# Cross attention's probability-value products as three fp16 products, their halves made by GpSimd and VectorE, on one Trainium2 core

## The reference

```python
x = _layernorm(x + self_attention(x))            # 8 heads of 16, biases, blocks of 64 tokens
x = _layernorm(x + cross_attention(x, ctx))      # 16 heads of 8, masked softmax, 64 keys
x = _layernorm(x + ffn(x))                       # 8 experts of 512, silu, top 2 by a router
```

```python
scores = jnp.einsum('bhqd,bhkd->bhqk', qh * SCALE, kh)
scores = jnp.where(mask[:, None, :, :], jnp.float32(-1000000000.0), scores)
attn = jax.nn.softmax(scores, axis=-1)
out = jnp.einsum('bhqk,bhkd->bhqd', attn, vh)    # the product that the change touches
```

## Time and profile before

| | us |
|---|---|
| median of 3 runs (lowest, highest) | 1054.99 (1054.93, 1057.35) |
| the profiled execution: its own time | 1055.75 |
| its span, first to last instruction | 1054.0 |
| PE busy | 897.6 (85%) |
| DVE busy | 790.4 (75%) |
| ACT busy | 711.0 (67%) |
| POOL busy | 429.1 (41%) |

### The profile page before, as it was taken

How to read it: one execution, slowest core, us unless ns; L and a number is a source line. 1 busy time by engine, 2 the same in 40 slices (tenths; PEclk the granted TensorE clock), 3 DMA queues, 4 the chain that set the end, 5 groups by cost and what they waited for, 6 DMA issues and landing times. The chain is left out here.

```text
span 1054.0 us, 30689 instructions
## 1 busy us (share of the span) xinstructions
PE 897.6 (85%) x11092; PEld 800.9 (76%) x11093; DVE 790.4 (75%) x2208; ACT 711.0 (67%) x1194; POOL 429.1 (41%) x527
## 2 busy tenths in 40 slices
PE   2898999898799989899898988893079999999990
PEld 1777777777588878788887877782079999999990
DVE  3688888888667887888887778777547777777771
ACT  3678777776577766767676756651058878878881
POOL 3133443344301110111212115565717777777773
PEclk9999999999799998999998989996589999999995
DMA  5960000000100000000000100010132332332210
GB/s 162 216 114 21 20 10 20 20 20 11 26 14 14 14 14 14 14 12 12 12 12 0 23 3 25 29 41 21 52 70 58 72 74 65 73 73 58 61 32 0
DMA packets 103725, 42.26 MB, mean 40 GB/s; under 512 B 58290, under 2 KB 99516, under 8 KB 103668
## 3 DMA queue, kind: packets, MB, share of 16 engines
q1 hardware_dynamic: 98676, 32.95, 15.0%
q0 software_dynamic: 4992, 8.54, 2.5%
HBM read 20.69 MB, written 16.57 MB: 35 GB/s over the span
## 5 line engine op out<-in xcount | busy, mean ns | idle before, releaser
L1118 DVE TENSOR_REDUCE mx<-psum 128x8 bf16<-128x512 f32 x192 | 132.2, 689 | 85.6 <-PE psum L539 82.7
L923 ACT ACTIVATE pr<-psum 128x512 f32<-128x512 f32 x192 | 114.2, 595 | 79.3 <-PE psum L618 78.9
L386 POOL TENSOR_SCALAR ve<-mv 128x4 f32<-128x4 f32 x55 | 15.8, 288 | 336.9 <-DVE mv L1276 322.9
L515 POOL DMA_INDIRECT out_dram<-X,dest x92 | 123.7, 1345 | 61.1 <-ACT X L1026 43.0
L627 PE MATMUL psum<-ident,pr 128*128 128x128 f32 x768 | 123.1, 284 | 29.7 <-ACT pr L923 29.6
L927 ACT ACTIVATE pt<-psum 128x512 f32<-128x512 f32 x192 | 113.8, 592 | 32.8 <-PE psum L627 32.1
L645 PE MATMUL psum<-vz_cross,pt 128*128 128x36 f32 x1024 | 130.8, 275 | 0.0
L645 PEld LDWEIGHTS psum<-vz_cross,pt 128*128 128x128 f32 x1024 | 129.3, 198 | 0.0
L627 PEld LDWEIGHTS psum<-ident,pr 128*128 128x128 f32 x768 | 88.0, 144 | 46.1 <-ACT pr L923 39.4
L1138 DVE TENSOR_TENSOR at<-psum,rc 64x64 f32<-64x64 f32 (+1 forms) x384 | 93.7, 244 | 7.2
L539 PE MATMUL psum<-wst,qz 128*128 128x128 f16 x512 | 98.2, 227 | 0.0
(11 more groups left out here) (224 smaller groups left out, 2964.4 us busy)
## 6 DMA issues: line engine op xcount, KB each, us to landing
xd<-blank SPq DMA_DIRECT2D x1, 6072.0 KB, 35.3
X<-xd SPq DMA_DIRECT2D x23, 264.0 KB, 2.9
X<-x_dram SPq DMA_DIRECT2D x16, 256.0 KB, 2.8
wst<-w_dram SPq DMA_DIRECT2D x16, 256.0 KB, 2.7
cin<-ctx_in_dram SPq DMA_DIRECT2D x16, 256.0 KB, 2.8
out_dram<-X,dest POOLq DMA_INDIRECT x92, 2.9
mraw<-mask_dram SPq DMA_DIRECT2D x32, 32.0 KB, 2.7
xd<-XTa,pos POOLq DMA_INDIRECT x64, 2.3
```

Source lines behind the costliest of these rows:

```text
L515: nc.gpsimd.indirect_dma_start(out=out_rows, out_offset=bass.IndirectOffsetOnAxis(ap=dest[i][:, k, 0:1].bitcast(U32), axis=0), in_=zo[i][k ...
L923: nc.scalar.activation(pr[u % 2][:], SC[u % 2][:], ACT.Exp).then_inc(s["ex"], 1)
L1118: nc.vector.tensor_reduce(mx[u % 2][:], SC[u % 2][:].rearrange("p (r k) -> p r k", k=S), AX.X, ALU.max).then_inc(s["mx"], 1)
```

## The change

1. In cross attention `values` becomes `three` over fp16 halves. POOL makes both halves of the probabilities from `pt`: per unit a cast to `pt_half[k][0]` and, after a wait for it, a subtraction into `pt_half[k][1]` (semaphores `pi`, `pl`). ACT's `vh` writes the high half of the values; DVE gets `vl`, four subtractions per group for the low one. `flip`, `values`, `XT` and `RT` wait for `pl` and `vl` where they waited for `ph` and `vh`.
2. POOL's other work of cross attention is placed by unit, behind the pair of that unit: `running` in pieces at 0 to 2, `low_rows` at 2, `ahead` at 3, `inv_std` at 6, `convert` at 7, and the sends one by one by a table.
3. `CHUNKS` becomes (0, 8, 12, 14, 16): sends begin in group 10; 31 are placed by the end of group 15 and 33 after it.
4. In self attention ACT's `vh` moves from unit 1 to unit 2.
5. Opening: x's first group is loaded second, PE's first transposes no longer wait for DVE's preparation, six of DVE's twelve preparing instructions are put behind the opening, and POOL copies x before it zeroes `vz`. The gates take 6 short DVE instructions in place of 8; DVE's closing is in another order.

```diff
-CHUNKS = (0, 10, 14, 16)
+CHUNKS = (0, 8, 12, 14, 16)
...
+                def cross_body(g, i, follow, p):
+
+                    known = isinstance(g, int)
+                    for u in range(la.nh):
+                        k = u % 2
+                        wait_apart(pool, s["ph"], g * la.nh + u + 1, pool_ready, POOL_READY)
+                        nc.gpsimd.tensor_copy(pt_half[k][0], pt[k][:]).then_inc(s["pi"], 1)
+                        pool.wait_ge(s["pi"], g * la.nh + u + 1)
+                        nc.gpsimd.tensor_tensor(pt_half[k][1], pt[k][:], pt_half[k][0], ALU.subtract).then_inc(s["pl"], 1)
+                        if i == 0 and not (known and g < 4) and u in COUNTING:
+                            running(p - 2, COUNTING[u])
+                        if u == slot(la, "HIGH") + 1 and not (known and g < 2):
+                            low_rows(g - 2)
+                        if u == slot(la, "HIGH") + 2 and follow >= 2:
+                            ahead(g + 2, i)
+                        if u == slot(la, "O") + 2 and not first_group(g):
+                            inv_std(g - 1, s["mv"], before, s["rs"])
+                        if u == slot(la, "FIN") and follow >= 2:
+                            convert(g + 2, i)
+                        if known and g >= first_tables:
+                            send(SENDS[g][u])
...
                 def flip(g, u, i):
                     n = g * la.nh + u
                     pe.wait_ge(s["ex"], n + 1)
-                    wait(pe, s["ph"], n - 1)
+                    wait(pe, s["pl" if la.cross else "ph"], n - 1)
...
-                    pe.wait_ge(s["ph"], n + 1)
+                    pe.wait_ge(s["pl" if la.cross else "ph"], n + 1)
...
+                        if la.cross:
+                            v = [w[:, bb % 2, (bb // 2) * la.quads + quad].rearrange("p j c d -> p (j c d)") for w in vz_half[i]]
+                            m = three(dst[:, b * W:(b + 1) * W], [w[:, c] for w in pt_half[u % 2]], v)
+                            continue
...
+                def vl(g, i):
+                    dve.wait_ge(s["vh"], g + 1)
+                    for b2_ in range(2):
+                        for jp in range(2):
+                            m = nc.vector.tensor_tensor(vdst(la, i, b2_, jp, 1), vsrc(la, b2_, jp), vdst(la, i, b2_, jp), ALU.subtract)
+                    m.then_inc(s["vl"], 1)
...
-SENT_BEFORE = {12: range(0), 13: range(4, 10), 14: range(15, 22), 15: range(28, 35)}
-SENT_AFTER = {12: range(0, 4), 13: range(10, 15), 14: range(22, 28), 15: range(35, 40)}
-SLOTS = {"self": {"QK": 0, "V": 1, "AT": 1, "O": 2, "XT": 3, "FIN": 3},
+COUNTING = {0: range(0, 3), 1: range(3, 6), 2: range(6, 8)}
+SEND_COUNTS = {10: (0, 0, 0, 0, 0, 0, 0, 1), 11: (1, 1, 0, 1, 1, 1, 0, 1), 12: (0, 0, 0, 1, 1, 1, 1, 1), 13: (1, 1, 0, 1, 1, 1, 1, 1),
+               14: (0, 0, 0, 1, 1, 1, 1, 1), 15: (1, 1, 0, 1, 1, 1, 1, 1), 16: (5, 4, 24)}
+SLOTS = {"self": {"QK": 0, "V": 1, "AT": 1, "O": 2, "XT": 3, "FIN": 3, "VH": 2},
```

More of the change, by code:

```diff
@@ L370, in _ @@
             for la in (SELF, CROSS):
-                for v in vz[la.name]:
+                for i in range(2):
+                    v = vz_half[i][0] if la.cross else vz[la.name][i]
                     for jp in range(2):
@@ L427, in send @@
                 for t in tiles:
+                    for c in range(NC):
+                        if t == chunk(c).start:
+                            pool.wait_ge(r_id, 1)
+                            pool.wait_ge(cleared, 16)
+                            pool.wait_ge(r_lr, CHUNKS[c + 1])
+                            pool.wait_ge(r_pos, sum(parts(k) for k in range(c + 1)))
                     if t % SEG == 0 and t >= 2 * SEG:
@@ L478, in groups @@
                     if la.cross:
+                        running(NPAIR - 2, range(PT))
                         low_rows(G - 2)
+                        send(SENDS[G][0])
                     inv_std(G - 1, s["mv"], before, s["rs"])
@@ L485, in _ @@
             next_opening, next_groups = attention(CROSS, G, None)
-            opening, groups = attention(SELF, 0, next_opening)
-            opening()
+            _, groups = attention(SELF, 0, next_opening)
             groups()
@@ L547, in XT @@
                     pe.wait_ge(s["xs"], g + 1)
-                    wait(pe, s["vh"], g)
+                    wait(pe, s["vl" if la.cross else "vh"], g)
                     if la.cross:
@@ L639, in values @@
                     if u == 0:
-                        pe.wait_ge(s["vh"], g + 1)
+                        pe.wait_ge(s["vl" if la.cross else "vh"], g + 1)
                     for b in range(HB):
@@ L743, in opening @@
                     XT(0, 0)
+                    pe.wait_ge(prep, PREP if la.cross else FIRST)
                     if la.cross:
@@ L1165, in body @@
                     ranked = la.cross and i == 0 and not (isinstance(g, int) and g < 4)
-                    tables = la.cross and isinstance(g, int) and g == first_tables
+                    c_now = table_of(g) if la.cross else None
+                    tables = c_now is not None
                     for u in range(la.nh):
@@ L1534 @@
     const[:, o:o + NP] = rows - 9 * E
-    steps = [np.append(np.diff(rows), last) for last in [rows[0] - rows[-1]] * 2 + [0]]
-    const[:, o + NP:o + 4 * NP] = np.concatenate(steps)
-    const[:, o + 4 * NP] = np.arange(P) * P
+    steps = [np.append(np.diff(rows), last) for last in [rows[0] - rows[-1]] * (NC - 1) + [0]]
+    const[:, o + NP:o + (NC + 1) * NP] = np.concatenate(steps)
+    const[:, o + (NC + 1) * NP] = np.arange(P) * P
     lanes = np.arange(NTILE)
```

207 lines of the change are left out of this document (110 added, 97 removed).

## The result

| | before | after |
|---|---|---|
| median (lowest, highest) | 1054.96 (1052.46, 1057.35), 4 runs | 1093.28 (1091.3, 1101.37), 4 runs |
| profiled execution, its span | 1055.75, 1054.0 | 1091.52, 1089.6 |

A forecast was written before the change was run, and what follows sets the result against it. PE was taken as the bound in cross attention's groups without select (24.12 of 24.8 us). Terms 14 + 19 + 3.5 - 9 - 5 + 1.5 = +24 gave 1079 us against the median, range 1037 to 1102.

The forecast's parts named there:

- PE saves: Cross attention's values: twelve fp16 pairs take 0.30 us a unit, saving PE 0.52 a unit, 4.2 a group, 67 over the stage.
- What stands in its place: Cross attention: probabilities go PE, ScalarE, GpSimd, PE; a round of two units without extras takes 4.9 us.
- The chain of 3.5 us: Cross attention: values of a unit starts at the earliest 3.5 us after its flip, where it was 1.3.
- The walk: One odd cross-attention group followed through PE's, ScalarE's and GpSimd's queues: period 26.1 us, 1.3 more than before.
- VectorE's holds: Cross attention: twelve classes and finish instructions a group meet GpSimd's pairs, 0.3 us each; VectorE reaches 25, just under the period.
- Another sign named ahead: Sign of being right: GpSimd busy for over 75% of cross attention, and nearly all of groups 11 to 15.
- Groups 0 to 9: Cross attention's first ten groups: five odd at +1.3 us, five even at +1.5, together +14.
- Groups 10 to 15: Cross attention's last six groups: sends at 1.26 us each beside GpSimd's pairs, together +19 us (between +8 and +28).
- After the last group: Stretch behind cross attention's last group: GpSimd's queue with 33 sends takes 51.6 us for 48.3, +3.5 (0 to +5).
- Self attention: Exponential no longer behind vh: 14 groups at 0.75 us, less a little for VectorE, -9 (0 to -10.5).
- Opening: Start of the kernel: PE's first projection comes at 11.6 us instead of 16.47, -5 (-4 to -6).
- Cross attention's opening: Start of cross attention: XT waits for vl too, +1.5 us.

The follow-up runs named there:

- with the delay and without the traffic: Changed kernel with GpSimd's subtraction replaced by a power on 128 x 4 elements, third product on the high half again: 1073.73 us, ratio 1.0171 to the kernel before.
- experiment 11: Changed kernel with all 64 sends put behind the last group: 1132.45 us, ratio 1.0732 to the kernel before.

## Why the prediction was right, and where it was wrong

**PE saves.** Right. The twelve pairs of 36 columns start (470.71 - 470.42)/11 = 0.026 us apart, and a unit's `values` takes 0.31 us, to 470.73, where the next product starts:

```profile
470.42 0.19 PE L567 MATMUL psum<-vz_cross,bhfull 128*128 128x36 f16 x1 [0.74 <-POOL Wf L495]
...
470.71 0.18 PE L569 MATMUL psum<-vz_cross,Wf 128*128 128x36 f16 x1
```

The row decides against the weight-load time of the Trainium skill (TensorE: Matmul & The Clock Gate, LDWEIGHTS and Weight-path perf modes), by which the prediction had worked out 0.64. PE's work in groups 0 to 9 fell by 246.2 - 216.6 = 29.6 us, 3.0 a group where 4.2 were taken; that part of `values` had lain over its neighbours before is likely, but no run tells it.

**What stands in its place.** The chain of 3.5 us is right (3.39; GpSimd started 0.13 after ScalarE, for 0.25). The walk gave a period of 26.1, and odd groups of the loop measured 25.9 to 27.9. But its mechanism was a third of the story: with the delay and without the traffic the same groups take 25.0 to 25.7, and groups 0 to 9 264.9, which is 5.1 of the 17.2 us lost. The prediction had put VectorE's holds at 0.3 us for each of twelve instructions and left them off the path, as VectorE's sum (25 a group; it measured 23.4) stayed under the period. They fall elsewhere, and heavier: in groups 0 to 9 `classes` average 367 and 452 ns, not over 500, while `finish` averages 774 (340 before), and its four come in front of a row maximum that PE waits for. That is the step that failed: a sum below the period was taken for proof that VectorE's place in the round does not matter. The traffic of the subtraction costs the first ten groups 12.6 us. Another sign named ahead failed as well: GpSimd was busy for 63% of groups 0 to 9 and 74% of groups 10 to 15, not for over 75%.

**Groups 0 to 9**, +17.2 for +14: the term is 3 short, for that reason. In even groups the held `finish` stands in front of `select` as well, and PE waits for the row maximum behind both. In group 8, where `finish` took 1.11 us before and PE's wait 3.18:

```profile
496.83 3.20 DVE L1337 TENSOR_SCALAR X<-z,mv,rstd 128x128 f32 x4
```

```profile
506.51 0.61 PE L648 MATMUL psum<-mx,negI 128*128 128x512 bf16 x1 [5.25 <-DVE mx L1158]
```

`finish` grew by 2.1 us and PE's wait by as much. Placing `running` in pieces costs something too: in groups 0 to 9 PE waits for its sums three times, 4.1 us together, and never did before. Group 8 grew by 3.9 us and group 7 by 2.2.

**Groups 10 to 15**, +20.8 for +19: right in size, wrong in cause. The sum was made of sends at 1.26 us each; experiment 11 prices all 31 at 5.2 at most. Groups 12 to 15 came within 1 us of what was computed for them (32.5, 29.2, 34.0, 27.2 for 33, 30, 33, 27), which shows how little an agreement of sizes proves.

**After the last group**, +6.9 for +3.5. GpSimd's sends are the bound and 9 more of them were counted rightly, but they start later: `finish` of group 14 waits 2.41 us for `inv_std`, which stood behind a pair, is held in turn, and `running` starts at 752.18, 7.2 us into the stretch; before, its second sum began 3.8 us in the earlier trace rows:

```profile
745.52 1.51 DVE L1337 TENSOR_SCALAR X<-z,mv,rstd 128x128 f32<-128x128 f32 x4 [2.41 <-POOL rstd L404]
```

```profile
752.18 0.22 POOL L441 TENSOR_TENSOR blow<-blow,vz_self 128x28 f16<-128x28 f16 x1 [2.30 <-issue]
...
799.27 0.96 POOL L453 DMA_INDIRECT xd<-XTa,pos  x1 [0.30 <-issue]
```

Measured from the last `flip`, the stretch is 50.6 before, 53.7 with the new send plan and no pair, and 57.6 with the pair: half and half.

**Self attention**, -13.9 for -9: two waits a group were covered by `vh`, one had been counted. **Opening**, +0.4 for -5: the steps of VectorE were priced by their rows of before, where the memsets had ended before they began; the new order lays them side by side, and one is held for 4.77 us. With the memsets moved, the first projection comes at 11.86, where 11.6 was computed. **Cross attention's opening**, +4.4 for +1.5: with self attention's last group it is 31.2 to 32.4 us in the kernels with the fp32 product, and 34.0 to 38.2 in those with the fp16 one; which of the waits makes that spread was not tried.

**The sum**, +36 for +24. Self attention and the opening missed by 5 us each, in opposite directions, and cancel; the other four terms all came out too small, by 11 together. That the whole stayed inside a range as wide as 1037 to 1102 is no test of the mechanism.

## What to carry to other kernels

Before work is put on GpSimd, look for what VectorE does at that time with its inputs in SBUF: its instruction ends with GpSimd's, and what counts is not the sum of VectorE's time but whether the held instruction stands in front of something that the bounding engine waits for. An engine's idle time in a round is no offer when the round must pass through the new work; here 30 us less of PE's work came with 47 us more of its waits in ten groups, 28 of them already there without the subtraction and 19 with it. And a forecast made of several terms is tested term by term: both stages of cross attention had the right size here for a partly wrong reason.

## What the runs showed of the hardware

- Beside GpSimd's cast or subtraction on 128 x 512 elements, a VectorE instruction with its tensor inputs in SBUF, `finish` or `classes`, was held until GpSimd's ended: `finish` takes 340 ns alone, 630 beside the cast (0.61 us) and up to 1323 beside the subtraction (1.16), and ends 80 ns after it; `classes` end 150 ns after it. Not every instruction is: in self attention of the changed kernel a `finish` at 103.57 us took 336 ns although it lay wholly beside a `tensor_scalar` of GpSimd's on 128 x 512 elements (1.51 us). Instructions with an input in PSUM (row maxima 0.69 us, `vl` 0.43) and `stats` (0.28) were not lengthened.
- GpSimd's length is not what counts: beside the power on 128 x 4 elements (1.01 us), `finish` took 341 ns.
- Memsets hold too, and several in a row are one hold: a `tensor_scalar` on 2 x 512 elements took 4.77 us beside the end of a copy and the memsets behind it, 0.72 without them. A `scalar_tensor_tensor` right behind it took 0.74 us beside shorter memsets, as long as with none.
- One kernel's groups 0 to 9 took 277.0 and 282.3 us in two executions. The granted clock was 0.97 and 0.95 and PE's work 5.4 us longer; VectorE's, ScalarE's and GpSimd's was the same within 0.3 us.
